# Top-16 search of a product-key layer: ranks above 8 taken from one list of 128 sums per head, after ScalarE has scaled and shifted both lists

## The reference

```python
s0 = jnp.einsum('bshq,eq->bshe', _l2norm(q0), _l2norm(keys0))      # 64 scores
s1 = jnp.einsum('bshq,eq->bshe', _l2norm(q1), _l2norm(keys1))      # 64 scores
sc0, ix0 = jax.lax.top_k(s0, K)                                    # K = 16
sc1, ix1 = jax.lax.top_k(s1, K)
cs = (sc0[..., :, None] + sc1[..., None, :]).reshape(b, s, H, K * K)
ci = (ix0[..., :, None] + ix1[..., None, :]).reshape(b, s, H, K * K)
fs, pos = jax.lax.top_k(cs, K)
fi = jnp.take_along_axis(ci, pos, axis=-1)
w = jax.nn.softmax(fs, axis=-1)
down = expert_down[fi]
up = expert_up[fi]
inner = jnp.einsum('bsd,bshkd->bshk', hidden_states, down)
act = jax.nn.gelu(inner, approximate=False)
out = jnp.einsum('bshk,bshko->bso', act * w, up)
```

## Time and profile before

| | |
|---|---|
| median of 3 runs | 1392.88 us (1389.09 to 1393.25) |
| the profiled execution | 1389.55 us, its span 1387.7 us |
| busy: PE, DVE, ACT, POOL | 1029.8, 1284.9, 919.2, 940.4 us |
| share of the span | 74%, 93%, 66%, 68% |
| mean granted TensorE clock | 0.759 of full speed |

### The profile page before, as it was taken

The page is one execution under the profiler, slowest core; times in us unless marked ns, Lnnn a source line. Parts: engine busy times, 40 slices in busy tenths (PEclk is TensorE's granted clock), DMA queues, the critical chain, the costliest instruction groups (busy, mean ns, idle before and its releaser), DMA issues.

```text
span 1387.7 us, 41186 instructions
## 1 busy us (share of the span) xinstructions
PE 1029.8 (74%) x9585; PEld 679.4 (49%) x9585; DVE 1284.9 (93%) x10050; ACT 919.2 (66%) x4155; POOL 940.4 (68%) x1947
## 2 busy tenths in 40 slices
PE   4767777877777777778778777786778878776753
PEld 2434554645455454555446454553545545463433
DVE  4349999999999989999899998999999999999995
ACT  2576867668586857858576784767658676766532
POOL 4438776786867768577677867676776777668552
PEclk7787786769788776878877696787868778685555
DMA  2100000000000000000000000000000000000000
GB/s 55 18 15 2 3 11 3 4 8 6 10 4 11 4 5 11 4 10 4 12 4 5 9 6 10 4 12 3 5 9 5 6 3 5 4 4 5 3 4 7
DMA packets 22512, 10.97 MB, mean 8 GB/s; under 512 B 13920, under 2 KB 22032, under 8 KB 22242
## 3 DMA queue, kind: packets, MB, share of 16 engines
q1 hardware_dynamic: 21618, 7.79, 2.5%
q10 hardware_dynamic: 624, 0.30, 0.1%
HBM read 4.58 MB, written 3.01 MB: 5 GB/s over the span
## 4 chain that ended last, share of the span: by engine, by line
DVE 60%; issue 15%; PE 8%; ACT 7%; POOL 6%; SPq 1%; DVEq 1%; DMA 0%; POOLq 0%; ACTq 0%
DVE idx L1466 14%; DVE val L1464 9%; DVE cr L1536 8%; DVE scores L1469 8%; DVE oh L1479 6%; DVE best L1534 4%; DVE wl L1499 3%; ACT ns_junk L863 2%; PE banks L1055 2%; DVE bns L1389 2%; DVE masked L1419 1%; POOL cs L623 1%; PE bankM L1219 1%; PE bankQ L1142 1%; ACT act_g L840 1%
## 5 line engine op out<-in xcount | busy, mean ns | idle before, releaser
L1466 DVE FIND_INDEX8 idx<-val,scores 124x8 uint16<-124x64 f32 x1536 | 304.4, 216 | 0.0
L1464 DVE MAX8 val<-scores 124x8 f32<-124x64 f32 x1536 | 210.6, 207 | 2.4 <-ACT scores L870 1.2
L1219 PE MATMUL bankM<-wl,oh 128*128 128x16 f16 x5952 | 162.8, 172 | 46.2 <-DVE wl L1499 46.2
L1219 PEld LDWEIGHTS bankM<-wl,oh 128*128 128x128 f16 x5952 | 160.0, 101 | 59.6 <-DVE wl L1499 33.2
L597 POOL TENSOR_TENSOR qscale<-nmx,power 124x16 f32<-124x16 f32 x48 | 147.8, 3079 | 45.4 <-DVE nmx L1443 45.3
L1469 DVE MATCH_REPLACE8 scores<-val,scores 124x64 f32<-124x64 f32 x768 | 151.4, 206 | 0.0
L863 ACT ACTIVATE ns_junk<-bankQ 124x32 f32<-124x32 f32 x768 | 138.0, 255 | 12.7 <-PE bankQ L1172 12.4
L1479 DVE TENSOR_SCALAR oh<-eh 128x992 f16<-128x992 int16 x384 | 135.2, 414 | 4.5 <-ACT eh L918 4.5
L863 ACT ACTIVATION_READ_ACCUMULATOR ns_junk<-bankQ 124x1 f32 x768 | 138.3, 268 | 0.0
L1108 PE MATMUL banks<-diag,probs 124*124 124x124 f32 x672 | 107.7, 327 | 25.0 <-ACT diag L808 25.0
L1227 PE MATMUL bankM<-up_x,prod 128*124 128x128 f32 x384 | 86.5, 396 | 50.5 <-DVE prod L1508 50.5
(11 more groups left out here) (196 smaller groups left out, 3067.8 us busy)
## 6 DMA issues: line engine op xcount, KB each, us to landing
x_in<-in_x SPq DMA_DIRECT2D x16, 93.8 KB
x_in<-in_x SPq DMA_DIRECT2D x16, 62.5 KB
out<-o_sb SPq DMA_DIRECT2D x16, 62.0 KB
out<-o_sb SPq DMA_DIRECT2D x16, 61.0 KB
out<-o_sb SPq DMA_DIRECT2D x16, 60.5 KB
x_in<-in_x SPq DMA_DIRECT2D x16, 31.0 KB
oh<-more SPq DMA_DIRECT2D x6, 54.0 KB
conv_w<-in_L_tok_kernel ACTq DMA_DIRECT2D x2, 128.0 KB, 3.2
```

The source lines that it names most:

```text
L1219: last = e.matmul(coef[:, g, :, :], oh[:, k, g, :, :].rearrange("p v t -> p (v t)"), wl[:, part, k, :, TG * g:TG * (g + 1)], start=k + par ...
L1464: last = v.max(out=v_[:, hd, s, best8], in_=src[:, hd, s, :])
L1466: last = v.max_index(out=i_[:, hd, s, best8], in_max=v_[:, hd, s, best8], in_values=src[:, hd, s, :])
```

## The change

Ranks above 8 of a list can only be in a cell with rank 0 of the other list: (a, 0) or (0, c) with a or c from 8 to 15. These 16 cells are no longer formed one by one.

- `rank` has only its steps 0 and 1: 8 values and indices per list.
- A new step `lift` (ACT) then rewrites the 64 scores of each list in place as score x `qscale` + the scaled best value of the other list. It is one ACTIVATE of 124 x 64 per list, with scale and bias read from SBUF per row, so 16 a tile, in two halves of 8. It waits for `val_s` of POOL (`vals_scaled`) and for `rank` of its half (`ranked`).
- A new step `late` (DVE) takes the 8 largest of the two lists of a head together (MAX8 over 128) straight into the last 8 cells of `cs`, and their positions (FIND_INDEX8 over 128) into `late_idx`: 8 and 8 a tile.
- Cells per head are 34 + 8 = 42 in place of 50. `choose`, `select`, `normalise`, `mark`, `cell_exp` and `weight_high` have 336 elements a row in place of 400.
- `index_floats` (ACT) is five small ACTIVATEs in place of one: the side of a late position, the indices, the late positions, the first index less 64, and the side as a float, with a semaphore between. `rank_sums` part 2 (POOL) has four more small operations and one fewer in each part.
- Lists, values and indices have three buffers (`ring(t)`).
- The orders of the four compute engines are written anew. The tables of cells that share a slot are new too.

```diff
+            def lift(c, t, half):
+                n = c.tile(t)
+                act.wait_ge(vals_scaled, 2 * n + 1 + half)
+                act.wait_ge(ranked, 8 * n + 4 * (half + 1))
+                for hd in range(4 * half, 4 * half + 4):
+                    for s in range(2):
+                        one = scores[c.ring(t)][:, hd, s, :]
+                        last = a.activation(one, one, ACT.Identity, scale=qscale[c.ring(t)][:, hd, s:s + 1], bias=val_s[c.ring(t)][:, hd, 1 - s, 0:1])
+                last.then_inc(lifted, 1)
             def index_floats(c, t):
-                act.wait_ge(ranked, 16 * (n + 1))
-                a.activation(idxf[c.slot(t)][:, :, :, :], idx[c.slot(t)][:, :, :, :], ACT.Copy, scale=1.0 / WSCALE).then_inc(idxf_ready, 1)
+                act.wait_ge(late_ready, 4 * (n + 1))
+                a.activation(side_i[:, :, :], late_idx[c.ring(t)][:, :, :], ACT.Identity, bias=side_bias[:, 0:1], scale=1.0 / PK).then_inc(sides_ready, 1)
+                a.activation(idxf[c.ring(t)][:, :, :, :], idx[c.ring(t)][:, :, :, :], ACT.Copy, scale=1.0 / WSCALE)
+                a.activation(late_f[c.ring(t)][:, :, :], late_idx[c.ring(t)][:, :, :], ACT.Copy, scale=1.0 / WSCALE)
+                a.activation(first_m[c.ring(t)][:, :], idx[c.ring(t)][:, :, 0, 0], ACT.Identity, bias=side_bias[:, 1:2], scale=1.0 / WSCALE)
+                act.wait_ge(sides_ready, n + 1)
+                a.activation(side_f[c.ring(t)][:, :, :], side_i[:, :, :], ACT.Copy).then_inc(idxf_ready, 1)
...
+            def late(c, t, half, step):
+                n = c.tile(t)
+                if step == 0:
+                    dve.wait_ge(lifted, 2 * n + 1 + half)
+                    wait(dve, exp_ready, n)
+                else:
+                    dve.wait_ge(late_ready, 4 * n + 2 * half + 1)
+                settled(dve, passed_dve)
+                for hd in range(4 * half, 4 * half + 4):
+                    both = scores[c.ring(t)][:, hd, :, :].rearrange("p s e -> p (s e)")
+                    if step == 0:
+                        last = v.max(out=cs[:, hd, INNER:NC], in_=both)
+                    else:
+                        last = v.max_index(out=late_idx[c.ring(t)][:, hd, :], in_max=cs[:, hd, INNER:NC], in_values=both)
+                last.then_inc(late_ready, 1)
...
             def body(c):
-                do(rank_sums, c, 0, 2)
-                do(q_scale, c, 1)
...
+                do(select, c, 0)
+                do(q_std, c, 2)
+                do(normalise, c, 0)
+                do(q_scale, c, 1)
                 do(p1_rstd, c + 1, 1)
```

More of the change, by code:

```diff
@@ L37, in together @@
         return (a + 1) * (c + 1) + (e + 1) * (g + 1) - (min(a, e) + 1) * (min(c, g) + 1) <= TOP
[L38 to L45, removed]
+    slots = SHARED + [[p] for p in CELLS if not any(p in cells for cells in SHARED)]
+    assert len(slots) + LATE <= SLOTS
     m = np.zeros((2 * NC, 2 * SLOTS), np.float16)
@@ L51, in merge_matrix @@
                 m[h * NC + CELLS.index(p), h * SLOTS + s] = 1
+    for k in range(LATE):
+        for h in range(2):
+            m[h * NC + INNER + k, h * SLOTS + SLOTS - LATE + k] = 1
     assert m.sum() == 2 * NC
@@ L604, in rank_sums @@
                 k = end - first
-                src, dst = (idxf[c.slot(t)], ce) if part == 2 else (val_s, cs)
+                src, dst = (idxf[c.ring(t)], ce) if part == 2 else (val_s[c.ring(t)], cs)
                 if part == 0:
-                    pool.wait_ge(ranked, 16 * n + 6)
+                    pool.wait_ge(ranked, 8 * n + 2)
                     wait(pool, chosen, 10 * n - 6)
                     wait(pool, exp_ready, n)
+                    wait(pool, lifted, 2 * (n - 2))
                 elif part == 1:
-                    pool.wait_ge(ranked, 16 * n + 14)
+                    pool.wait_ge(ranked, 8 * n + 6)
                 else:
@@ L672, in body @@
                 do(p1_rstd, c + 2, 0)
+                do(rank_sums, c, 1, 2)
+                do(rank_sums, c, 2, 0)
                 do(select, c, 1)
-                do(q_scale, c, 2)
+                do(normalise, c, 1)
                 if at(c, -2):
@@ L971, in body @@
                 do(q_squares, c + 1, 0)
+                do(q_scores, c, 2)
+                do(index_floats, c, 1)
                 if at(c, -1):
@@ L1551, in body @@
             def body(c):
-                do(p1_res, c)
-                do(product, c + -2, 2)
-                do(p1_stats, c, 1)
-                do(rank, c + -1, 1, 0, 2)
-                do(p1_moments, c, 1)
-                do(rank, c + -1, 1, 0, 3)
-                do(rank, c + -1, 1, 1, 0)
                 if at(c, -1):
                     key_norms()
+                do(finish, c + -2, 2)
                 do(p1_shift, c, 1)
-                do(finish, c + -2, 2)
+                if at(c, 0):
+                    split_bias()
@@ L1598, in body @@
-                if at(c, 0):
-                    for step in range(4):
-                        rank(c, 0, 0, step)
-                if at(c, -1):
-                    centred_weights()
+                do(late, c + -1, 2, 0, 0)
+                do(late, c + -1, 2, 1, 0)
+                do(late, c + -1, 2, 0, 1)
+                do(p1_smax, c + 1, 0)
+                do(late, c + -1, 2, 1, 1)
                 do(choose, c + -1, 2, 0)
@@ L1607, in body @@
                 do(one_high, c + -1, 1, 0)
-                do(p1_smax, c + 1, 0)
                 do(one_low, c + -1, 1)
+                if at(c, 0):
+                    for step in range(2):
+                        rank(c, 0, 1, step)
                 do(one_high, c + -1, 1, 1)
@@ L1618, in body @@
                 do(p1_rden, c + 1, 1)
-                do(invert_sums, c + -1, 2)
-                do(p1_smax, c + 1, 2)
-                if at(c, 0):
-                    for step in range(4):
-                        rank(c, 0, 1, step)
-                if not at(c, 0):
-                    do(rank, c, 0, 0, 2)
-                if not at(c, 0):
-                    do(rank, c, 0, 0, 3)
                 if not at(c, 0):
```

275 lines of the change are left out of this document (154 added, 121 removed).

## The result

The changed kernel takes 1503.11 us (median of 4 runs, 1501.96 to 1506.61) against 1393.07 us of the kernel before beside it: a ratio of 1.080, 95% interval 1.077 to 1.083. It is 110 us slower; 1452 us was forecast. The profiled execution took 1501.96 us, with a span of 1500.2 us.

A forecast was written before the change was run, and what follows sets the result against it. DVE was taken to bound the kernel before, ACT the changed one: 15 batches x (84.2 - 79.7) = +68 us, -8 at the end, 1389.55 to 1450, median 3.3 above: 1452 us; forecast range 1415 to 1490 (0.58).

The forecast's parts named there:

- The bound moves from DVE to ACT: Per batch, ACT's work rises from 55.7 to 73.8 us, above DVE's, which falls to 71.9 us.
- The walk: One loop body of all engines followed in the new order: 73.8 us ACT work plus waits, 84.2 us a batch.
- The wait ahead of `cells_T`: ACT at `cells_T(c, 0)` stands still 2.4 us for POOL's second part, PE's 12 turns and two crossings.
- The waits at `late`: DVE stands still 10 to 12 us a batch, as a half's lift follows its last MATCH_REPLACE8 and takes 2.7 us.
- the gap at the top of the loop adds up to 1 us where DVE's `p1_moments` is on this chain: DVE's gap ahead of `p1_res` at the loop's top adds at most 1 us to the walk; 84.2 us was taken.
- it gets worse than my walk: Rival, chance 0.12: PE's clock falls or the loop gap hits ACT's chain in full; 87.5 us a batch, about 1500 us.
- the ends, -8 us: At the end, some 1.5 batches without first-layer work stay bound by DVE: -8 us.
- DVE's 92 us: DVE's searches and `choose` save 1.92 us a tile, 5.8 a batch, 92 us in 48 tiles.
- A cheap lift: Rival, chance 0.14: a lift costs under 0.34 us; at 0.20 about 1350 us, cheaper still about 1300.
- Waits that overlap better: Rival, chance 0.16: ACT's waits are 5 us, not 9.6, giving some 1384 us; with 7, about 1415.
- A lower clock of PE: Part of the 0.12 worse case: PE's clock, 0.77 on average, falls and its longer products lengthen the waits.
- The rule for VectorE: Skill's rule: multiply and add on VectorE; lifts there cost 2.3 us a tile, 80.8 us a batch, some 17 us more.

## Why the prediction was right in sign and mechanism, and short in size

**The bound moves from DVE to ACT: as forecast.** The rows of two, eight and sixteen lifts, and the load put alone into the kernel before, show it. The lift was forecast at 0.34 us and took 0.348. `late` was forecast at 0.201 and 0.262 us: from start to start MAX8 over 128 takes 0.20 and FIND_INDEX8 0.26, with tails 0.217 and 0.266. ACT was forecast at 1190 to 1220 us and had 1183.5, and the batch at 83 to 86 and took 86.2, both just outside; DVE, at 1185 to 1200, had 1242.8.

**The walk: 84.2 us a batch, near but for the loop, in part by luck.** Without the loop a batch took (1324.5 - 57.3)/15 = 84.5. ACT works some 72.4 us of it, where I had 73.8, and stands still 12, where I had 10.4: two errors that mostly cancel. The wait ahead of `cells_T` was in the right place and too small, 3.87 us against 2.4: my walk let PE turn the cells as soon as POOL had written them, and PE was still behind its scatter. The waits at `late` were forecast at 10 to 12 us a batch. They are 101.8 us in 46 times, 6.4 a batch.

**The step that failed first: "the gap at the top of the loop adds up to 1 us where DVE's `p1_moments` is on this chain".** The 84.2 us that I took counted next to nothing for it. The loop costs the changed kernel 86.2 - 84.5 = 1.7 us a batch, 25 in all, of the 51 by which the forecast was short. I had read one gap; the trace of before has a second of 7.4 us in 4 times ahead of `prod`, and 8.6 + 7.4 = 16.0 is just what the kernel before gained without its loop. I had also put its full effect on ACT's chain only into the rival "it gets worse than my walk", at 87.5 a batch and some 1500 us. This was the case that came, at 86.2, though that rival had DVE's gap alone, and PE has one as well.

**The step that failed second: the ends, -8 us.** I let the last one and a half batches stay bound by DVE. Measured, in spans:

| | forecast | measured |
|---|---|---|
| 15 batches | +68 | 15 x 6.5 = +97 |
| up to the first `p1_res` | 0 | 55.4 - 49.2 = +6.2 |
| behind the last `p1_res` | -8 | 151.8 - 142.5 = +9.3 |
| together | +60 | +112.5 |

With two lifts a tile the part behind the last `p1_res` takes 1386.5 - 1246.5 = 140.0 us, with the load alone in the kernel before 1593.2 - 1440.1 = 153.1, so ACT's load lengthens the end as it does the middle. The 6 us at the start stay in every version of the new order, with two lifts too (56.7 us), and do not come with the load alone (49.5 us). ACT waits there once, 13.6 us, ahead of its first `convT`; its longest wait there was 6.2 before. Which line of the new order does that was not tried.

**The step that did not decide, but was wrong: DVE's 92 us.** Its busy time fell by 42. By its groups, one MAX8 and one FIND_INDEX8 a list are gone with 106.6 and 150.8 us, those over 128 take 83.4 and 102.3, and `choose` takes 13 less: a saving of 85, and the term was 7 too large by the tails of the wide ones. Some 24 us net are other operations that became longer: in the groups of the changed kernel

```profile
L1541 DVE TENSOR_SCALAR oh<-eh 128x992 f16<-128x992 int16 x384 | 148.8, 450 | 2.2 <-ACT eh L958 2.2
...
L1552 DVE TENSOR_TENSOR ol<-el,lows 128x992 f16<-128x992 int16 x48 | 41.7, 869 | 1.6
```

against 135.2 and 33.0 us before, and 12.7 against 7.9 for `nmx`. The rest, 19 us, stays open. With two lifts, when DVE waits less, the busy time is 7 us lower, so a part may be tails that nothing overlaps in a wait.

**The rivals.** *A cheap lift*, 0.14, was priced wrong even if it had come: I gave 1350 us at 0.20 each and 1300 for nothing, and 2 of 16 lifts still took 1388.6. So by that run even nearly free lifts were no faster than before in this form. *Waits that overlap better* did not come. *A lower clock of PE* came, 0.75 in the stretch above against 0.77, and its share of the time is open. *The rule for VectorE* was priced at some 17 us over before and measured at 159: DVE's own work became 83.2 us a batch, not 80.8, and it still waited 5.9. Why it waits is not shown; that POOL and ACT now get its results later is a guess.

## What to carry to other kernels

When work moves from a full engine to one that is half idle, price it against the idle time that is left in the right places, not against the sum: here 270 us of lifts met 470 us of idle time and 110 came out on the clock. A short experiment tells beforehand that it will cost, if not how much: the load alone in the old kernel, with nobody waiting for it, came out at 203 us against the change's 110. And look for stalls with "issue" as their reason at a loop's top on every engine: writing the loop out gained 16 us in one kernel and 25 in the other, and was the only edit that brought a kernel with all its work below the kernel before.

## What the runs showed of the hardware

- At the top of a loop over two batches DVE stood 2.45 and 1.94 us without a releaser (17.3 us together in the trace: 9.6 in 4 times and 7.7 in 5), with only two instructions between. With the bodies written out both gaps were gone.
- A plain DVE operation can wait for POOL's. In the changed kernel POOL's and DVE's timelines show

```profile
723.39 1.25 POOL L662 TENSOR_TENSOR wcell<-taken,ce 124x336 f16<-124x336 f16 x1 [1.28 <-issue]
724.60 1.08 POOL L664 TENSOR_TENSOR wsel<-taken,cx 124x336 f32<-124x336 f16 x1
```

```profile
723.87 0.80 DVE L1489 TENSOR_TENSOR nmx<-nss,qguard 124x16 f32<-124x16 f32 x1
724.59 2.03 DVE L1541 TENSOR_SCALAR oh<-eh 128x992 f16<-128x992 int16 x4
```

`nmx`, 16 elements wide and 0.17 us in the median, ends as POOL's `wcell` ends, and the four `oh` beside `wsel` take 2.03 us where they take 1.39 with POOL elsewhere. The Trainium skill (SBUF — State Buffer, SBUF: two separate sides) says that GpSimd and some of VectorE's operations hold one pair of ports in turn and block each other; these rows agree with it. That the new order set them more often side by side is read from the groups, and was not tested by itself.
- Eight lifts of 64 elements took 2.76 us with scale and bias read per row, 0.345 each; eight squares of 64 with a constant scale took 1.59 with their accumulator reads the earlier trace rows. That the operands per row make the difference is not shown, since the squares also read PSUM; a copy of 256 elements between SBUF tiles with a constant scale took 0.33 us, less than a lift of 64.
